# VectorE work is reordered around a sort's loop, and the first 31 gather indices are made apart, in a graph network kernel

## The reference, cut to what matters

```python
def _conv(x, row, col, edge_type, edge_weight, W, b):      # row = src, col = dst
    deg = segment_sum(ones, col)
    norm = deg_inv_sqrt[row] * deg_inv_sqrt[col] * edge_weight
    xw = jnp.einsum('ni,tio->tno', x, W)                   # 4 types: a table of 4 rows per node
    x_j = xw[edge_type, col] * norm[:, None]               # gather a row per edge
    out = segment_sum(x_j, row) + b                        # add up by row: wants edges sorted by row
    return leaky_relu(out, 0.01)
z1 = _conv(x, ...); z2 = _conv(z1, ...); z3 = _conv(z2, ...)
```

## Time and profile before

| | us |
|---|---|
| median of 3 runs | 8987.56 |
| lowest and highest | 8986.87, 8988.84 |
| the profiled execution | 8985.63 |
| its span, first to last instruction | 8983.9 |
| POOL busy in the span | 6418.4 (71%) |
| PE, DVE, ACT busy | 5647.1, 4620.3, 3966.1 |

### The profile page before, as it was taken

How to read it: one execution, slowest core, us unless ns; L and a number is a source line. 1 busy time by engine, 2 the same in 40 slices (tenths; PEclk the granted TensorE clock), 3 DMA queues, 4 the chain that set the end, 5 groups by cost and what they waited for, 6 DMA issues and landing times.

```text
span 8983.9 us, 149271 instructions
## 1 busy us (share of the span) xinstructions
PE 5647.1 (63%) x32763; PEld 4282.7 (48%) x32764; DVE 4620.3 (51%) x12880; ACT 3966.1 (44%) x12195; POOL 6418.4 (71%) x6527
## 2 busy tenths in 40 slices
PE   4885555555556555555556555555555777777775
PEld 3664444444444444444444444444444666666665
DVE  9995232323234232322324232322326999999998
ACT  5552232323223232322323232322325888888887
POOL 0666777777776777777776777777775777777775
PEclk9996555555556555555556555555555787787877
DMA  1001111111114111111113111111112333334333
GB/s 51 33 34 54 53 53 53 53 53 53 53 54 105 53 53 53 53 53 53 53 53 102 53 53 53 53 53 53 53 53 69 115 116 115 116 115 116 115 115 93
DMA packets 432674, 612.42 MB, mean 68 GB/s; under 512 B 232025, under 2 KB 249478, under 8 KB 432526
## 3 DMA queue, kind: packets, MB, share of 16 engines
q0 software_dynamic: 208832, 428.96, 17.2%
q1 hardware_dynamic: 223694, 182.02, 6.4%
HBM read 437.29 MB, written 51.28 MB: 54 GB/s over the span
## 4 chain that ended last, share of the span: by engine, by line
issue 26%; POOL 25%; DMA 23%; DVE 18%; DVEq 4%; PE 4%; ACT 0%; POOLq 0%; ACTq 0%; SPq 0%
POOL g_rows L722 25%; DMA g_rows<-gcn_table,rec_idx 22%; DVEq L1547 3%; DVE a_miss L1662 2%; DVE a_max L1667 1%; DVE state L1720 1%; DVE lo_hot L1233 1%; DVE acc L1726 1%; DVE v_hot L1373 1%; DVE a_lo L1746 1%; DVE a_sum L1690 1%; DVE state L1680 1%; DVE a_drop L1708 1%; DVE a_left L1741 1%; PE wide L1131 1%
## 5 line engine op out<-in xcount | busy, mean ns | idle before, releaser
L722 POOL DMA_INDIRECT g_rows<-gcn_table,rec_idx x4836 | 4586.1, 948 | 1546.4 <-issue 1215.7
L900 ACT ACTIVATE g_step<-g_rows,rec_w 128x128 f32 x5580 | 1781.2, 389 | 4160.3 <-POOLq L702 3875.3
L1167 PE MATMUL bank<-g_step,g_hot 128*128 128x128 f32 x7440 | 1851.4, 427 | 1589.8 <-ACT g_step L900 1492.2
L1167 PEld LDWEIGHTS bank<-g_step,g_hot 128*128 128x128 f32 x7440 | 1592.6, 316 | 2020.2 <-issue 2020.2
L1577 DVE TENSOR_TENSOR acc<-acc,bank 128x512 f32 x930 | 639.5, 688 | 2700.7 <-PE bank L1167 2697.8
L747 POOL DMA_INDIRECT a_roll<-gat_table,src_plane x1612 | 1525.2, 946 | 494.4 <-issue 445.3
L1167 PE MATMUL wide<-g_step,g_hot 128*128 128x128 f32 x3720 | 925.8, 427 | 854.1 <-ACT g_step L900 831.4
L1167 PEld LDWEIGHTS wide<-g_step,g_hot 128*128 128x128 f32 x3720 | 795.9, 316 | 1068.7 <-issue 1068.7
L925 ACT ACTIVATE a_cand<-a_miss,a_rows 128x128 f32<-128x128 bf16 x3608 | 1096.0, 386 | 19.8 <-DMA a_rows<-a_roll 19.8
L1577 DVE TENSOR_TENSOR acc<-acc,wide 128x512 f32 x465 | 319.7, 688 | 1424.9 <-PE wide L1167 1423.2
L1563 DVE TENSOR_TENSOR g_hot<-bank,rec_lo 128x512 f32<-128x512 f32 x1395 | 952.2, 683 | 1.8 <-DVE mv L1621 0.2
(11 more groups left out here) (263 smaller groups left out, 5014.9 us busy)
## 6 DMA issues: line engine op xcount, KB each, us to landing
a_rows<-a_roll SPq DMA_DIRECT2D x451, 264.0 KB
g_rows<-gcn_table,rec_idx POOLq DMA_INDIRECT x4836
gcn_table<-rows SPq DMA_DIRECT2D x147, 256.0 KB
a_roll<-gat_table,src_plane POOLq DMA_INDIRECT x1612
e_dst<-by_dst_dst SPq DMA_DIRECT2D x451, 2.0 KB
gat_table<-acc SPq DMA_DIRECT2D x7, 462.0 KB
out_x<-xs SPq DMA_DIRECT2D x6, 448.0 KB
gcn_slots<-nothing SPq DMA_DIRECT2D x4, 468.0 KB, 5.7
```

The lines of the kernel that those rows point to most:

```text
L722: pool.indirect_dma_start(out=g_rows[:, tile % RING, :], out_offset=None, in_=gcn_tables[layer % 2], in_offset=bass.IndirectOffsetOnAxis(a ...
L900: last = nc.scalar.activation(g_step[:, j, k, :].unsqueeze(1), g_rows[:, bass.ds(slots[k], 1), :], ACT.Copy, scale=rec_w[:, bass.ds(q.at(0 ...
L1167: last = nc.tensor.matmul(sums_of(j)[:, bass.ds(places[k], D)], g_hot[:, j % 3, k, :], g_step[:, j % 3, k, :], start=False, stop=(k == GP ...
```

## The change

On VectorE the marks and the check move behind the sort's loop, five of the attention lists' seven ops behind the listing; the record codes, `gat_base` and `gat_need` move into its passes -3, -2 and -1, behind the `hot` of each. TensorE's wait for `s_count` 3 moves from ahead of the loop to behind it, ScalarE's wait for `s_vals` into its pass -1 ahead of the first copy of values. In quarter 0, TensorE first makes the indices of 31 columns apart (`bank[3]`, `s_flip0`), VectorE copies them (`keep_first`, in the middle of `decode(0)`), and POOL's first 31 gathers wait for `s_idx0` alone; the other 372 columns are made as before, and POOL waits for them ahead of gather 32. Tiles of the sort get other places in SBUF, since codes are now live together with them. The diff, cut to its core:

```diff
@@ -252,29 +252,28 @@
         tmp_f = sb("tmp_f", [P, COLS], F32, head)
+        src_lo = sb("src_lo", [P, COLS], I32, head)
         dst_lo = sb("dst_lo", [P, COLS, 2], BF16, head)
-        src_lo = sb("src_lo", [P, COLS], I32, head)
+        lo_hot = sb("lo_hot", [P, 2, HIST, P], BF16, head)
         tally = ExitStack()
-        lo_hot = sb("lo_hot", [P, 2, HIST, P], BF16, tally)
         hi_hot = sb("hi_hot", [P, 2, HIST, BW], BF16, tally)
...
         passed = sb("passed", [NB, 2, GAT.groups], F32, head)
-        gat_group = sb("gat_group", [1, 2, GAT.groups], F32, head)
         head.close()
         spans = ExitStack()
-        hot = sb("hot", [P, SORT.ring, SPAN, BW], BF16, spans)
         v_hot = sb("v_hot", [P, 2, 16, PARTS, BW], BF16, spans)
         p_hot = sb("p_hot", [P, 2, 16, P], BF16, spans)
+        run = sb("run", [BW, SORT.ring, P * PARTS], BF16, spans)
+        packed = sb("packed", [P, PARTS * BW], BF16, spans)
+        val2 = sb("val2", [P, 2, SPAN, PARTS, 2], BF16, spans)
+        hot = sb("hot", [P, SORT.ring, SPAN, BW], BF16, spans)
         upto = sb("upto", [BW, 2, SPAN], F32, spans)
...
         pos = sb("pos", [P, 2, SPAN, 2], BF16, spans)
-        val2 = sb("val2", [P, 2, SPAN, PARTS, 2], BF16, spans)
-        packed = sb("packed", [P, PARTS * BW], BF16, spans)
-        run = sb("run", [BW, SORT.ring, P * PARTS], BF16, spans)
         spans.close()
@@ -315,6 +314,7 @@
...
+        gat_group = sb("gat_group", [1, GAT.groups], F32, listing)
...
@@ -708,7 +709,9 @@
                     c, u = divmod(q, CSPANS)
-                    if u == 0 and not layer:
+                    if q == 0 and not layer:
+                        pool.wait_ge(s_idx0, 1)
+                    if (q == 1 or c and u == 0) and not layer:
                         pool.wait_ge(s_idx, c + 1)
@@ -806,6 +808,8 @@
                     w = q.slot(1) % 2
+                    if q.i is None and q.base == -1:
+                        act.wait_ge(s_vals, 1)
                     if q.live(-1):
@@ -1013,7 +1017,6 @@
             pass_groups()
-            pe.wait_ge(s_count, 3)
             pe.wait_ge(s_in["w"], 64)
@@ -1078,6 +1081,7 @@
             pe.wait_ge(s_ranked, len(GROUPS) * SORT.steps)
+            pe.wait_ge(s_count, 3)
             list_steps()
@@ -1093,6 +1097,12 @@
                     pe.wait_ge(s_field, 2 * c + (2 if n else 1))
+                    if use == 0:
+                        for k in range(4):
+                            last = nc.tensor.matmul(bank[3][:, 0:TURN], field[:, 0, 0, k * P:(k + 1) * P],
+                                                    sel[:, k, 0:TURN], start=(k == 0), stop=(k == 3))
+                        last.then_inc(s_flip0, 1)
+                    skip = TURN if use == 0 else 0
                     if use >= 8:
@@ -1102,7 +1112,7 @@
                         if n == 0:
-                            last = nc.tensor.matmul(ps[:, 0:CCOLS], part, sel[:, 4 * c + k, :],
+                            last = nc.tensor.matmul(ps[:, skip:CCOLS], part, sel[:, 4 * c + k, skip:],
                                                     start=(k == 0), stop=(k == 3))
@@ -1314,13 +1324,8 @@
             chain(V.tensor_scalar(block_step[:, :], block_i[:, :], bin_no[:, 0:1], None, ALU.add))
-            for c in range(CH):
-                chain(V.tensor_scalar(ended[:, c, :], iota_n[0:NB, :], block_step[0:NB, c:c + 1], None, ALU.is_ge))
             chain(V.scalar_tensor_tensor(block_at[:, :], bin_at[:, :], float(P), bank[7][0:BW, 0:CH],
                                          ALU.mult, ALU.add))
-            chain(V.tensor_tensor(start_diag[:, :, :], spread(ident[0:BW, 0:BW].unsqueeze(1), [BW, CH, BW]),
-                                  spread(block_at[:, :].unsqueeze(2), [BW, CH, BW]), ALU.mult))
-            dve.sem_inc(s_count, 1)
             chain(V.tensor_copy(at_f[:, 0:1], block_at[:, 0:1]))
@@ -1329,38 +1334,30 @@
             codes = vals[:, :, :].bitcast(U16)
-            dve.wait_ge(s_in["weight"], 48)
             halves = w_f[:, :].bitcast(U16).rearrange("p (c h) -> p c h", h=2)
             top = tmp_f[:, :].bitcast(U16)[:, 0:COLS]
-            dve.wait_ge(s_in["type"], 48)
-            chain(V.tensor_copy(codes[:, 0, :], halves[:, :, 1]))
-            chain(V.tensor_scalar(codes[:, 1, :], dst_i[:, :], float(NB * P - 1), float(MARK), ALU.min, ALU.add))
-            chain(V.tensor_scalar(codes[:, 3, :], halves[:, :, 0], MARK - 1, MARK, ALU.bitwise_and, ALU.bitwise_or))
-            chain(V.tensor_scalar(top, halves[:, :, 0], 3, 7 << 10, ALU.logical_shift_right, ALU.bitwise_and))
-            chain(V.scalar_tensor_tensor(type_i[:, :], type_i[:, :], float(P), top, ALU.mult, ALU.add))
-            chain(V.tensor_scalar(src_lo[:, :], src_i[:, :], P - 1, MARK, ALU.bitwise_and, ALU.bitwise_or))
-            chain(V.tensor_tensor(codes[:, 2, :], type_i[:, :], src_lo[:, :], ALU.add))
-            dve.sem_inc(s_vals, 1)
-
-
-            dve.wait_ge(s_in["next"], 16)
-            chain(V.tensor_tensor(tmp_f[:, 0:COLS - 1], dst_f[:, 0:COLS - 1], dst_f[:, 1:], ALU.is_gt))
-            chain(V.tensor_reduce(falls[:, 0:1], tmp_f[:, 0:COLS - 1], AX.X, ALU.max))
-            chain(V.tensor_copy(falls[:, 1:2], dst_next[:, :]))
-            chain(V.tensor_tensor(falls[:, 2:3], dst_f[:, COLS - 1:], falls[:, 1:2], ALU.is_gt))
-            chain(V.tensor_tensor(falls[:, 3:4], falls[:, 0:1], falls[:, 2:3], ALU.max))
-
-
-            dve.wait_ge(s_planned, 3)
-            begun = bank[0][:, 0:GAT.groups]
-            chain(V.tensor_scalar(gat_block[:, :], begun[0:1, :], -1.0, None, ALU.add))
-            chain(V.tensor_scalar(gat_base[:, :], begun, float(P), -float(P), ALU.mult, ALU.add))
-            chain(V.scalar_tensor_tensor(gat_group[:, 0, :], iota_n[0:1, 0:GAT.groups], 1.0, begun[0:1, :],
-                                         ALU.add, ALU.subtract))
-            chain(V.tensor_scalar(gat_group[:, 0, :], gat_group[:, 0, :], float(GAT_GROUPS - 1), None, ALU.min))
-            chain(V.tensor_copy(gat_at[:, :, 0], gat_group[:, 0, :]))
-            chain(V.tensor_scalar(gat_at[:, :, 1], gat_at[:, :, 0], ROLL - 1, None, ALU.bitwise_and))
-            chain(V.tensor_tensor(gat_need[:, :], iota_n[0:1, 0:GAT_GROUPS], bank[1][0:1, 0:GAT_GROUPS], ALU.add))
+
+            def plan_groups():
+                dve.wait_ge(s_planned, 3)
+                chain(V.tensor_scalar(gat_base[:, :], bank[0][:, 0:GAT.groups], float(P), -float(P), ALU.mult, ALU.add))
+                chain(V.tensor_tensor(gat_need[:, :], iota_n[0:1, 0:GAT_GROUPS], bank[1][0:1, 0:GAT_GROUPS], ALU.add))
+
+            def code_weights():
+                dve.wait_ge(s_in["weight"], 48)
+                chain(V.tensor_copy(codes[:, 0, :], halves[:, :, 1]))
+                chain(V.tensor_scalar(codes[:, 1, :], dst_i[:, :], float(NB * P - 1), float(MARK), ALU.min, ALU.add))
+
+            def code_rest():
+                chain(V.tensor_scalar(codes[:, 3, :], halves[:, :, 0], MARK - 1, MARK, ALU.bitwise_and, ALU.bitwise_or))
+                dve.wait_ge(s_in["type"], 48)
+                chain(V.tensor_scalar(top, halves[:, :, 0], 3, 7 << 10, ALU.logical_shift_right, ALU.bitwise_and))
+
+            def code_sources():
+                chain(V.scalar_tensor_tensor(type_i[:, :], type_i[:, :], float(P), top, ALU.mult, ALU.add))
+                chain(V.tensor_scalar(src_lo[:, :], src_i[:, :], P - 1, MARK, ALU.bitwise_and, ALU.bitwise_or))
+                chain(V.tensor_tensor(codes[:, 2, :], type_i[:, :], src_lo[:, :], ALU.add))
+                dve.sem_inc(s_vals, 1)
+
             V.memset(most[:, :], 0.0).then_inc(s_at, 1)
@@ -1392,6 +1389,13 @@
                     one_hot(hot[:, k3, :, :], src_hi[:, span, :], iota_b).then_inc(s_keys, 1)
+                if q.i is None and q.base == -3:
+                    plan_groups()
+                    code_weights()
+                if q.i is None and q.base == -2:
+                    code_rest()
+                if q.i is None and q.base == -1:
+                    code_sources()
                 if q.live(0):
@@ -1445,6 +1449,19 @@
             run_steps(dve, SORT, 5, 3, body)
+            for c in range(CH):
+                chain(V.tensor_scalar(ended[:, c, :], iota_n[0:NB, :], block_step[0:NB, c:c + 1], None, ALU.is_ge))
+            chain(V.tensor_tensor(start_diag[:, :, :], spread(ident[0:BW, 0:BW].unsqueeze(1), [BW, CH, BW]),
+                                  spread(block_at[:, :].unsqueeze(2), [BW, CH, BW]), ALU.mult))
+            dve.sem_inc(s_count, 1)
+
+            dve.wait_ge(s_in["next"], 16)
+            falling = w_f[:, 0:COLS - 1]
+            chain(V.tensor_tensor(falling, dst_f[:, 0:COLS - 1], dst_f[:, 1:], ALU.is_gt))
+            chain(V.tensor_reduce(falls[:, 0:1], falling, AX.X, ALU.max))
+            chain(V.tensor_copy(falls[:, 1:2], dst_next[:, :]))
+            chain(V.tensor_tensor(falls[:, 2:3], dst_f[:, COLS - 1:], falls[:, 1:2], ALU.is_gt))
```

(18 more changed lines are left out.)

4 lines of the change are left out of this document (2 added, 2 removed).

## The result

| | before | after |
|---|---|---|
| median of 15 runs each, us | 8988.84 (8986.46 to 8993.17) | 8970.11 (8967.73 to 8971.84) |
| profiled execution, us | 8985.63 | 8968.89 |
| its span, us | 8983.9 | 8967.1 |

The ratio is 0.9979, with a 95% interval of 0.9972 to 0.9986: 18.7 us less, where 21.0 were forecast, and 8970.11 stands where 8966.6 was forecast. The interval leaves out 1, so the kernel is faster, if by little. The spans of the two profiled executions differ by 16.8 us, and this is what can be followed in the traces (8968.89 stands where 8964.6 was forecast for the profiled one).

The account below looks back on a forecast made before the run. POOL's gathers lead the chain, so only the first gather's time (716.31 us) could count: 15.7 + 5.9 - 0.6 = 21.0 us less, profiled 8964.6, median 8966.6. Own range 8964 to 8969; with rivals A to D, 8962.5 to 8973.

Parts of the forecast that it names:

- part four: Behind the loop, first 31 indices: made apart by eight small matmuls (1.3 us), they let POOL's gathers start 5.9 us earlier.
- parts one and two: Ahead of the loop and passes -3 to -1: 19.6 us leave, 10.2 come back partly hidden in waits; gain 15.7.
- From there on VectorE has no wait: From pass 0 to the loop's end: VectorE never waits, before and now, so the 15.7 us gain is carried through.
- rival D: Behind the loop: TensorE's clock shifts and L1008's 6.50 us of matmuls run at full clock, 3.2 better, 8963.4; chance 0.04.
- Part three: Behind the loop: the marks moved there lose 0.2 us; the check, 4.3 us, hides beside TensorE's L1000 and L1002.
- Later cost: From the first gather on: gathers slowed by eight more us of VectorE overlap, 0.6 us taken, 0.8 at most.
- Rival B: Behind the loop: last scatter, held beside the check, lands records up to 5.1 us later; 8971.7, or 8969 with slack; chance 0.07.
- C: First 31 indices: making them apart gives nothing, as small matmuls are slow or gathers held up elsewhere; 8972, chance 0.05.
- E: In the loop: the scatter's chain becomes the bound and each step grows; 9034 at 2 us more per scatter, chance 0.03.

Follow-up runs that it names:

- fills_ahead: Changed kernel, clamped, with all the fills (plans and record codes) back ahead of the loop: 0.9994 of before, first `v_hot` at 217.9 us.
- check_ahead: Changed kernel, clamped, with the check of destinations back ahead of the loop: 0.9992 of before, first gather at 699.6 us.
- before_again: Kernel before with only the waited-on tile number clamped at 0, the follow-up runs' baseline: 1.0007 of before, first gather at 715.3 us.
- early_tiles: `both`, plus the check's matmul ahead of the sum of starts and decoding without waiting for the begun-blocks count: 0.9983 of before, first gather at 689.9 us.
- loop_only: Changed kernel, clamped, without the first 31 indices made apart: 0.9985 of before, first gather at 704.7 us.
- first_only: Kernel before, clamped, with the first 31 indices made apart and nothing moved in the loop: 0.9998 of before, first gather at 712.2 us.
- busy_fill: Changed kernel, clamped, with matmuls that compute nothing put on TensorE in the three passes ahead of the loop: 0.9976 of before, first gather at 695.6 us.
- after_again: Changed kernel run again with only the clamp added: 0.9991 of before, first gather at 695.9 us.
- after_third: Same kernel as after_again, run once more: 0.999 of before, first gather at 695.1 us.
- one_matmul: Changed kernel, clamped, with the first 31 indices made by one matmul rather than four and copied earlier: 0.9978 of before, first gather at 694.7 us.
- both: Changed kernel, clamped, with the edits of plan_moved and one_matmul together: 0.9974 of before, first gather at 692.3 us.
- plan_moved: Changed kernel, clamped, with group plans and the source mark moved into pass -2: 0.9975 of before, first gather at 692.6 us.

## Why the prediction was right, and where it was off

The moved work and the first gather's time are what the prediction said, and the traced sum is 16.4 - 3.1 + 4.3 - 0.85 = 16.8 us, where 15.7 + 5.9 - 0.6 = 21.0 stood. Missing are 3.1 for the waits in the loop, 1.0 for the count and 0.6 for a term of part four, with 0.2 more given back later, against 0.7 that parts one and two gave more than forecast. The first two go with TensorE's clock. The measured median, 8970.11, lies 1.1 above the forecast's own range (8964 to 8969) and inside the wider one (8962.5 to 8973), whose upper part was there for rivals that are out. That the medians differ by 18.7 and not by 16.8 was not followed.

- **Parts one and two** (forecast 15.7; measured 16.4 in the trace, of which 0.55 lie ahead of all that was changed). The second `hot` was forecast at 190.95 and came at 190.34; the first `picked` at 197.5 and came at 196.92 behind a wait of 3.03; the next at 206.2 and came at 205.61 with none. All three are 0.6 early, by the 0.55. What the fills hide was tested by fills_ahead, and the step holds: the passes cost 3.8 of the 10.2, where 3.9 were forecast.
- **"From there on VectorE has no wait"** failed in the profiled execution, by 3.1 us. The step that was wrong is that the loop's time was taken as one number, with TensorE's clock only in rival D and only behind the loop. What the runs show in its place: TensorE's granted clock falls to half 10 to 14 times from 200 us to the loop's end in every one of the fourteen traces, mostly for 3.4 us, which VectorE hardly feels (one wait of 0.2 us in check_ahead); four traces have one of 10.2 or 13.7 us early in the loop (the table), and in three of these VectorE waits for 1.8 to 3.1 us. Without a long one the loop takes the old 464.9 to 465.3.
- **Part three** (loss of 0.2, check hidden). The check is hidden (check_ahead). The count started 4.3 us behind the last `v_hot` where it was 4.0: a loss of 0.3, and 0.2 was forecast. But it took 5.3 and not 4.4, by its place against the clock. At a quick count the check itself is last by 0.2.
- **Part four** (5.9 with the 0.2 taken off; 4.3 in the trace, 5.5 by the rest, 6.1 forecast). The mis-sized term is the eight small matmuls, forecast at 1.3 and measured at 1.89: 0.6. What else is missing from the 5.9 is the count, 0.9 longer and 0.1 later than was forecast.
- **Later cost** 0.6, measured 0.85.
- **Rival B.** The scatter beside the check took 0.92. The one ahead of it took 1.70; it was held by the loop's own `v_hot`, as its like in before_again was (1.05), and not by the check. The Trainium skill ("SBUF — State Buffer", section "Who interferes with whom") says that a VectorE op with two SBUF inputs contends with a GpSimd op that reads SBUF; the hold behind the bf16 `v_hot` agrees, and the check's TENSOR_REDUCE, beside which 0.92 was taken, is an op that the section has as free. The section also infers that such a two-input op leaves the making of a DMA's descriptors alone; the held scatters speak against that for a scatter by indices. The check's wide two-input op had no scatter beside it in any trace, so the rule is not tested on it.
- **Rival D** had the clock in it, and it came out the other way: the half-clock matmuls behind the loop took 6.50 in 13 traces of 14 (6.44 in early_tiles), at half clock each time; what the clock moved was the count ahead of them and the loop. Even at full clock they would give little alone, as the records land when they end (early_tiles).
- **C and E** are out: part four gives over 5, and the loop's step is the old one.

What stays open is what starts a long fall, and so how many of the 15 runs of the changed kernel had one. Idle time of TensorE alone does not do it. In all four traces with a long fall TensorE stood idle for 2.4 to 2.9 us just ahead of it or at its start (221.7 to 224.0 in after, 222.1 to 224.5 in loop_only, 238.3 to 240.6 in first_only, 204.7 to 207.6 in busy_fill); but it stood as long from 221.4 to 223.9 in before and from 204.1 to 207.8 in after_again, and no long fall followed. In after_again, after_third, one_matmul and `both` a short fall began at 219 to 221 us, and the idle time at 222 is not there: at half clock TensorE was still at work then. No run took the idle time away and left the rest, so its part is not shown.

## What to carry to other kernels

Work put into the waits of a pipeline's filling is hidden to the size of each wait, pass by pass; a wait that was covered by the list ahead of it has to be counted too, since it is what comes late next. Count the slack that an off-path engine has at half of its clock and not at the clock of the profiled execution, wherever its work is within a few us of the bound. Where a load waits for a flag that goes through other engines' queues, the places of its two small instructions (0.19 and 0.14 us long) in the queues moved the load by 1.4 us. Look too for a second bound that ends at the same moment: by the trace of `both` the earlier load alone would have gained next to nothing, though that was not run.

## What was not expected of the hardware

- TensorE's granted clock falls at places that differ between executions of one kernel: after_again at 221 to 224, after at 225 to 239. The 32 count matmuls, of the same shapes, took from 3.5 to 5.3 us by it.
- A scatter that is issued beside the last `v_hot` (bf16, two SBUF inputs) ends 0.8 us behind it, however early it started: issued at 677.76 beside a `v_hot` that ends at 678.65 it takes 1.70 and ends at 679.46; in before_again 1.05, from 691.61, behind an end at 691.86.
- The median length of the 4836 gathers is 944 ns in some executions and 947 in others. From the first gather on, plan_moved, at 944, takes 8269.9 us, and `both`, at 947, 8286.3 on the same chip:

```profile
L725 POOL DMA_INDIRECT g_rows<-gcn_table,rec_idx x4836: 940/944/6761, 692.6 to 6805.2; - x194
```

```profile
L725 POOL DMA_INDIRECT g_rows<-gcn_table,rec_idx x4836: 943/947/6765, 692.3 to 6817.2; - x194
```

  That is 16 us, as much as the whole change. It fits that on this chip the kernel before took 8987.0 once and 8999.6 to 9004.57 in the other 28 runs, and plan_moved 8964.3 once (the profiled one) and 8976.4 to 8982.6 in the other 8; what sets the length is not known. The comparison of this document has 944 on both sides.
- On two of three chips GpSimd waited 1456 and 1572 us for ScalarE ahead of the layers' gathers (before_again and after_third), and the program takes a third longer. In the profile of before the largest waits there are "issue" with 1215.7 and the gathers' own landings with 256.3. ScalarE's own wait there is put down by the trace to "remote" and "issue"; the cause was not found.

```profile
POOL g_rows L722 <- ACT g_step L899: 1456.3, 190, 26.6
```
